# Second and third tile of each sequence: value product directly ahead of the next scores, output projection behind QKV, lower part of the output on GpSimd

## The chip, the core and the metric

The kernel runs on one core of one Trainium2 chip. The metric is the device time of one execution in microseconds (us), and several executions give a median. The engines are TensorE (PE in the rows; PEld are its weight loads), VectorE (DVE), ScalarE (ACT), GpSimd (POOL) and the DMA queues, of which SyncE (SP) issues nearly all.

## The reference

Eight sequences of 512 rows and 256 columns go through a two-layer transformer block, a linear recurrence (a fast-weight learner with a delta rule), and the same transformer block again. The change touches the transformer layers only, and there the attention half:

```python
def _layer(x, wqkv, qs, ksc, wo, lg, lb, w1, b1, w2, b2):
    h = shift_token(x)
    q, k, v = jnp.split(h @ wqkv, 3, axis=-1)        # 8 heads of 64
    q = l2norm(q) * qs
    k = l2norm(k) * ksc
    q, k = rotary_xpos(q, k)
    o = local_attention(q, k, v)                     # window 128, looks one window back
    x = x + o.transpose(0, 2, 1, 3).reshape(b, n, INNER) @ wo
    h = shift_token(x)
    h = layernorm(h) * lg + lb
    a, g = jnp.split(h @ w1 + b1, 2, axis=-1)
    x = x + (a * gelu(g)) @ w2 + b2
    return x
...
x = x + 0.5 * ffn(layernorm(x))
x = x + attn(layernorm(x))
x = x + 0.5 * ffn(layernorm(x))
```

## The kernel before

**Passes and tiles.** Four layer passes (two layers, run twice) go over eight sequences, so 32 sequence passes; between the second and the third layer stands the recurrence, which the change leaves alone. A sequence is four tiles of 128 rows, t = 0 to 3, called first to fourth tile here. Every large product is made with operands split into a high and a low part and three products (`split_product`, L1181): high by high, high by low, low by high.

**Order.** Nothing schedules the kernel: each engine has its own program, written out by hand in a function `sequence` (PE L1445, ACT L962, DVE L2073, POOL L686), and semaphores tie them. An engine does its steps strictly in that order, so an instruction that waits holds up all that stands behind it on its engine. While TensorE works on tile t of a sequence, it also prepares tile t+1 ("ahead") and the input of tile t+2, and between these steps it fills in the second feed-forward product of the sequence before (`W2`, 17 units of one 128x256 product for each tile, cut into pieces by the table `cuts`).

**TensorE, second to fourth tile.** Scores `S` (L1255, 48 products of 64x64 quarters of the array); output projection `WO` of the tile before (L1183 to L1185 with `wo`, 12 products into bank 6); QKV of the tile ahead, `A1` (18 products into banks 0, 1 and 2); transposes of the probabilities `PT` and `PTE` (L1275, L1282); 7 units of `W2` (L1441); transposes of the input, `A0` (L1195); the value product `PV` (L1306, 64 products on quarters of the array, into banks 6 and 4); transposes of q and k of the tile ahead, `A2` (L1228; q first, which waits for `qrot`, then k, which waits for `krot`); 10 units of `W2`. In the fourth tile `H2T` (L1345, L1351: transposes of the normalized rows) and the fourth `WO` follow, and then the first feed-forward product `W1`, 132 products.

**VectorE, second to fourth tile.** `W2` (L1999, the residual of the sequence before); `O` (L1907, the low part of the output of the tile before); `S` (L1879, the scores with mask, scale and row minimum), with the reciprocals `R`; for the tile ahead rotary and its sum for k (L1841, L1845, L1852) and the sum of squares of k (L1866); `WO` (L1914: adds the projection in bank 6 to the residual and releases `xa_done`, for which `PV` waits, since it writes bank 6 again); the sum of squares of q, rotary for q and its sum (L1852 again, which releases `qrot`); `halves` (L1933, L1934: statistics of the tile before); `A0` (L1817); `O_add` (L1901: adds the two halves of the value product). In the fourth tile `LN_moments` (L1949, L1947, L1953) and `halves` stand behind `WO`, ahead of the squares of q, and `LN_apply` (L1961, L1965), `O`, `W2`, `H2T` and `WO` of the fourth tile behind `O_add`.

**ScalarE** copies the transposed probabilities (L866, L875), the halves of the output (`O_first` L885) and its high part (`O` L899), q and k (L847, L835), and makes the exponentials (L856). **GpSimd** multiplies the probabilities with the reciprocals (`NP` L642) and k with its norm (`A1_k` L629, which releases `krot`), makes powers (L626, L637, L674), and adds the bias (`XB` L659).

## Time and profile before

| | us |
|---|---|
| median of 3 runs | 2507.77 (2507.73 to 2510.44) |
| the profiled execution | 2504.67 |
| its span, first to last instruction | 2502.8 |
| PE busy in it | 2460.8 (98%) |
| DVE busy | 1972.0 (79%) |
| ACT busy | 1813.8 (72%) |
| POOL busy | 1561.5 (62%) |

The granted clock of TensorE is 0.999 of its full 2.4 GHz over the span. A matmul's record is longer than the time it takes of the engine, since the products are pipelined: what counts is from one start to the next. A timeline row gives the start of a group of like instructions, its length, the number in it, and, in brackets, how long the engine had stood idle before it and what ended that.

### The profile page before, as it was taken

Reading aid. Unit: us, or ns where it says so; the run is one execution under the profiler, and the core shown is the slowest. Engines: PE = TensorE matmul, PEld = TensorE weight load, DVE = VectorE, ACT = ScalarE, POOL = GpSimd, SP = SyncE. Lnnn points to the kernel's source line nnn. Section 1 sums busy time; section 2 is a strip of 40 time slices with the busy share of each in tenths; the row PEclk is TensorE's granted clock in tenths of the full one; section 3 lists DMA queues with packets and bytes.
Section 4 is the critical chain, followed back from the end, with each engine's and each line's share of the span. In section 5 each row is a group of like instructions: output and inputs, shape, how many; then the busy total and the mean of one; then the engine's idle time right before and its main releaser. Section 6 shows DMA issues by size and latency. Waiting matters only on the chain. (4 is left out here: it accounts for less than half of the span.)

```text
span 2502.8 us, 80310 instructions
## 1 busy us (share of the span) xinstructions
PE 2460.8 (98%) x29664; PEld 2208.2 (88%) x29664; DVE 1972.0 (79%) x6501; ACT 1813.8 (72%) x5232; POOL 1561.5 (62%) x1799
## 2 busy tenths in 40 slices
PE   8999999999999999999999999999999999999999
PEld 7899989999999999998766899999999989999998
DVE  7788888877878887777656888777777788888886
ACT  6777777777777777776554777777777777777776
POOL 6566667666666676665212666666666667666665
PEclk9999999999999999999999999999999999999999
DMA  3121111003000000005101000000003100000000
GB/s 128 36 86 56 37 58 56 27 24 121 15 3 2 3 2 28 2 4 211 36 19 35 2 3 2 3 2 2 2 2 124 36 2 19 19 19 19 19 19 27
DMA packets 75957, 82.21 MB, mean 33 GB/s; under 512 B 37552, under 2 KB 61872, under 8 KB 74416
## 3 DMA queue, kind: packets, MB, share of 16 engines
q1 hardware_dynamic: 74272, 75.61, 9.3%
q8 instruction: 238, 3.90, 0.6%
q10 hardware_dynamic: 1296, 1.46, 0.2%
q14 instruction: 151, 1.24, 0.2%
HBM read 49.53 MB, written 26.74 MB: 30 GB/s over the span
## 5 line engine op out<-in xcount | busy, mean ns | idle before, releaser
L642 POOL TENSOR_TENSOR pr<-pr,rden 128x384 f32<-128x384 f32 (+1 forms) x480 | 409.4, 870 | 275.7 <-DVE rden L1888 270.4
L856 ACT ACTIVATE pr<-pr,nb 128x192 f32<-128x192 f32 (+1 forms) x1024 | 438.0, 430 | 169.7 <-DVE nb L1879 169.7
L1183 PE MATMUL bank<-h2T,w 128*128 128x256 f32 x1344 | 386.1, 287 | 2.7
L1184 PE MATMUL bank<-h2T,w 128*128 128x256 f32 x1344 | 376.8, 280 | 0.0
L1185 PE MATMUL bank<-h2T,w 128*128 128x256 f32 x1344 | 376.8, 280 | 0.0
L1879 DVE CUSTOM_DVE_ANT_0 pr<-bank,maskb,r 128x192 f32<-128x192 f32 (+1 forms) x1024 | 347.0, 393 | 25.9 <-POOL r L637 11.8
L684 POOL TENSOR_TENSOR uTl<-t,uTh 128x256 fp32r<-128x256 f32 x288 | 217.8, 760 | 182.3 <-ACT uTh L956 149.1
L1183 PE MATMUL bank<-wqkv,hT 128*128 128x512 f32 x768 | 304.5, 397 | 1.8 <-DVE nb L1879 1.8
L1184 PE MATMUL bank<-wqkv,hT 128*128 128x512 f32 x768 | 302.7, 394 | 0.0
L1185 PE MATMUL bank<-wqkv,hT 128*128 128x512 f32 x768 | 299.8, 390 | 0.0
L1983 DVE SCALAR_TENSOR_TENSOR t<-bank,b,t 128x256 f32<-128x256 f32 (+1 forms) x384 | 184.4, 480 | 108.5 <-POOL uTl L684 46.2
L1183 PEld LDWEIGHTS bank<-h2T,w 128*128 128x128 f32 x1344 | 253.9, 189 | 8.1 <-issue 5.8
L1184 PEld LDWEIGHTS bank<-h2T,w 128*128 128x128 f32 x1344 | 257.1, 191 | 0.0
L1185 PEld LDWEIGHTS bank<-h2T,w 128*128 128x128 f32 x1344 | 252.6, 188 | 0.0
L1441 PE MATMUL bank<-w2h,uTh 128*128 128x256 f32 (+1 forms) x768 | 225.6, 294 | 2.3 <-issue 2.3
L1441 PE MATMUL bank<-w2l,uTh 128*128 128x256 f32 (+1 forms) x768 | 224.9, 293 | 0.0
L674 POOL TENSOR_TENSOR rs<-vare,small 128x4 f32<-128x4 f32 (+2 forms) x96 | 95.1, 991 | 204.4 <-DVE vare L1953 204.2
L637 POOL TENSOR_TENSOR r<-ssg,small 128x8 f32<-128x8 f32 x128 | 213.1, 1665 | 10.7
L626 POOL TENSOR_TENSOR r<-ssg,small 128x8 f32<-128x8 f32 x128 | 213.2, 1665 | 8.0
L1255 PE MATMUL bank<-kT,qT 64*64 64x64 f32 (+2 forms) x6656 | 207.9, 264 | 6.4 <-ACT kT L835 3.1
L941 ACT ACTIVATE t<-bank,b 128x256 f32<-128x256 f32 x320 | 150.6, 471 | 81.2 <-PE bank L1185 77.8
L1255 PEld LDWEIGHTS bank<-kT,qT 64*64 64x64 f32 x6656 | 184.5, 133 | 25.6 <-ACT kT L835 5.4
(256 smaller groups left out, 7122.4 us busy)
## 6 DMA issues: line engine op xcount, KB each, us to landing
wqkv<-wqkv_split SPq DMA_DIRECT2D x18, 512.0 KB, 6.3
w<-w_split SPq DMA_DIRECT2D x3, 2816.0 KB, 9.8
Y<-in_x SPq DMA_DIRECT2D x8, 512.0 KB, 8.2
stt<-stt SPq DMA_DIRECT2D x256, 3.0 KB
out<-Y SPq DMA_DIRECT2D x8, 512.0 KB, 3.8
h<-out SPq DMA_DIRECT2D x7, 512.0 KB, 3.9
out<-h SPq DMA_DIRECT2D x7, 512.0 KB, 3.0
stt<-stt SPq DMA_DIRECT2D x192, 0.0 KB
```

The costliest lines, as they stand in the source:

```text
L626: e.tensor_tensor(r[:, t, 0, :], ssg[:, 0, :], minus_half, ALU.pow).then_inc(rk_done, 1)
L637: e.tensor_tensor(r[:, t, 1, :], ssg[:, 1, :], minus_half, ALU.pow).then_inc(rq_done, 1)
L642: e.tensor_tensor(probs(j, t), probs(j, t), rden[:, 2 * j:2 * j + 2].unsqueeze(2).to_broadcast([P, 2, w]), ALU.mult).then_inc(pn_done, 1 i ...
L684: e.tensor_tensor(uTl[:, half, JOBS[i], :], ut[:, job % 2, :], uTh[:, half, JOBS[i], :], ALU.subtract).then_inc(u_lo, 1)
L856: last = e.activation(probs(j, t)[:, g, :], probs(j, t)[:, g, :], ACT.Exp, bias=nb[:, hd:hd + 1], scale=-1.0, accum_out=den[:, hd:hd + 1])
L1183: e.matmul(out, left[0], right[0], start=first, stop=False)
L1184: e.matmul(out, left[0], right[1], start=False, stop=False)
L1185: return e.matmul(out, left[1], right[0], start=False, stop=last)
L1255: m = e.matmul(out[:, to:to + w, :], qT[rows, 0, p, HB * a:HB * a + HB], kT[rows, p, block:block + w, :], start=True, stop=True, skip_grou ...
L1441: mm = e.matmul(bank[bk][:, 0:D], left, right, start=(unit == 0), stop=(unit == UNITS - 1))
L1879: m = e.tensor_tensor_reduce(probs(j, t)[:, g, :], bank[j][:, g * 256:g * 256 + w], far, r[:, t, 1, place(hd):place(hd) + 1], FAR, ALU.add ...
L1983: e.scalar_tensor_tensor(ut[0:rows, job % 2, :], bank[job % 4][0:rows, 0:256], b1[0:rows, L % 2, 0, mt:mt + 1], gg[0:rows, job % 2, :], AL ...
```

## The change

It is made in the second and third tile (t = 1, 2) and, in part, in the fourth (t = 3).

- TensorE: `PV` of the second and third tile goes from ahead of `A2` to behind it, so that the next tile's scores follow it. The fourth stays where it is. `WO` of the second and third tile goes from ahead of QKV to behind it, ahead of `PT` (the first tile's stays ahead). The 17 units of `W2` are cut anew: second tile 17 between `PTE` and `A0` (before 7, and 10 behind `A2`); third tile 6 between scores and QKV and 11 behind `PTE`; fourth tile 6 between scores and QKV, 2 behind `PTE` and 9 behind `A2`.
- ScalarE: `O_first` of the second and third tile behind the copies of q and k.
- VectorE: `O_add` of the second and third tile from the end of its tile to the start of the next, where the low part `O` stood. `WO` of the second and third tile from ahead of the squares of q to behind the sum of rotary for q; `halves` of the third tile with it.
- GpSimd: new function `O_lower` makes the low part of the output of the second and third tile, ahead of `NP`.

```diff
@@ -673,6 +673,13 @@
                 e.wait_ge(s_pln, at(s_pln, 3 * b + (24 * L + part + 1)))
                 e.tensor_tensor(rs[:, half, lo:hi], vare[:, half, lo:hi], small[:, 0:1].to_broadcast([P, hi - lo]), ALU.pow).then_inc(rs_done, 1)
 
+            def O_lower(L, b, t):
+                n = idx(L, b, t)
+                for i in pair:
+                    e.wait_ge(o_hi, at(o_hi, 2 * n + i + 1))
+                    e.tensor_tensor(oT[:, 1, 2 * i:2 * i + 2, :].rearrange("p a c -> p (a c)"), o_sum[:, 2 * P * i:2 * P * i + 2 * P],
+                                    oT[:, 0, 2 * i:2 * i + 2, :].rearrange("p a c -> p (a c)"), ALU.subtract).then_inc(o_lo, 1)
+
             def zero_rest():
 
                 e.memset(uTh[:, :, MT - 1, :].bitcast(F32), 0.0).then_inc(s_zero, 1)
@@ -690,6 +697,8 @@
                         XB(*prev, t)
                     if prev and t == 0:
                         U_last(*prev)
+                    if t > 1:
+                        O_lower(L, b, t - 1)
                     for j in range(4 if t else 3):
                         if t == 0 and j == 2:
                             guard_k(*ahead)
@@ -979,13 +988,14 @@
                         PTE(L, b, t)
                     if ahead2:
                         A0(*ahead2)
-                    if t:
+                    if t == 3:
                         O_first(L, b, t)
-                    if t == 3:
                         O(L, b, t)
                     if ahead and t:
                         A2_q(*ahead)
                         A2_k(*ahead)
+                        if t < 3:
+                            O_first(L, b, t)
                     elif ahead:
                         A2_k(*ahead)
                         A2_q(*ahead)
@@ -1446,7 +1456,7 @@
                 for t in range(NT):
                     ahead = (L, b, t + 1) if t < NT - 1 else nxt and (*nxt, 0)
                     ahead2 = (L, b, t + 2) if t < NT - 2 else nxt and (*nxt, t - 2)
-                    cuts = ((5, 6, 11, 13, UNITS), (0, 0, 7, UNITS), (0, 0, 7, UNITS), (0, 0, 7, UNITS))[t]
+                    cuts = ((5, 6, 11, 13, UNITS), (0, 0, UNITS, UNITS), (0, 6, UNITS, UNITS), (0, 6, 8, UNITS))[t]
 
                     def fill(k):
                         if prev and cuts[k] < cuts[k + 1]:
@@ -1456,8 +1466,8 @@
                         W2(*prev, t, 0, cuts[0])
                     S(L, b, t, 0, bool(nxt))
                     S(L, b, t, 1, bool(nxt))
-                    if t:
-                        WO(L, b, t - 1)
+                    if t == 1:
+                        WO(L, b, 0)
                     fill(0)
                     if L == 0 and b == 0 and t:
                         beta((5, 4, 6)[t - 1])
@@ -1466,6 +1476,8 @@
                     else:
                         e.wait_ge(nb_done, at(nb_done, 4 * idx(L, b, t) + 1))
                         busy(14, 0)
+                    if t > 1:
+                        WO(L, b, t - 1)
                     for j in range(4):
                         if not ahead and j > 1:
                             busy(4, 0)
@@ -1475,13 +1487,15 @@
                     fill(1)
                     if ahead2:
                         A0(*ahead2)
-                    if t:
+                    if t == 0:
+                        PV_first(L, b, t)
+                    if t == 3:
                         PV(L, b, t)
-                    else:
-                        PV_first(L, b, t)
                     if ahead and t:
                         A2(*ahead, 1)
                         A2(*ahead, 0)
+                        if t < 3:
+                            PV(L, b, t)
                     elif ahead:
                         A2(*ahead, 0)
                         fill(2)
@@ -2076,8 +2090,11 @@
                     ahead2 = (L, b, t + 2) if t < NT - 2 else nxt and (*nxt, t - 2)
                     if prev and t:
                         W2(*prev, t - 1)
-                    if t:
-                        O(L, b, t - 1)
+                    if t == 1:
+                        O(L, b, 0)
+                    elif t:
+                        for i in pair:
+                            O_add(L, b, t - 1, i)
                     S(L, b, t, 0)
                     S(L, b, t, 1)
                     S(L, b, t, 2)
@@ -2110,22 +2127,24 @@
                         if ahead:
                             rotated(*ahead, 0)
                             squares(idx(*ahead), 0)
-                        WO(L, b, t - 1)
+                        if t == 1:
+                            WO(L, b, 0)
                         if t == 3:
                             LN_moments(L, b, 0)
-                            halves(L, b, t - 1)
                         if ahead:
                             squares(idx(*ahead), 1)
                             rotary(*ahead, 1)
                             rotated(*ahead, 1)
                         if L == 0 and b == 0 and t == 3:
                             beta()
-                        if t < 3:
-                            halves(L, b, t - 1)
+                        if t > 1:
+                            WO(L, b, t - 1)
+                        halves(L, b, t - 1)
                         if ahead2:
                             A0(*ahead2)
-                        for i in pair:
-                            O_add(L, b, t, i)
+                        if t == 3:
+                            for i in pair:
+                                O_add(L, b, t, i)
                     if L == 0 and b < 2 and t == 1:
                         entry_stats(b + 1, 2)
                         entry_stats(b + 1, 3)
```

The names in the order rows are the program's: bank is PSUM, `ident,t` the transposes of q (waits `qrot`) and k (waits `krot`), `pT,v` the value product, `kT,qT` the scores, w2h, w2l, uTh, uTl the units of `W2`.

TensorE in the second tile of a sequence of the first layer, behind the transposes of the input, before:

```order
L1306 MATMUL bank<-pT,v 64x128 [waits pt_sb,xa_done]
L1306 MATMUL bank<-pT,v 64x128 x7
L1306 MATMUL bank<-pT,v 64x128 [waits pt_sb]
L1306 MATMUL bank<-pT,v 64x128 x7
L1306 MATMUL bank<-pT,v 64x64 [waits pt_sb]
L1306 MATMUL bank<-pT,v 64x64 x15
L1228 MATMUL bank<-ident,t 128x128 [waits qrot]
L1228 MATMUL bank<-ident,t 128x128 x3
L1228 MATMUL bank<-ident,t 128x128 [waits krot]
L1228 MATMUL bank<-ident,t 128x128 x3
L1441 MATMUL bank<-w2l,uTh 128x256
L1441 MATMUL bank<-w2h,uTl 128x256
```

And in the changed kernel, at the same place:

```order
L1238 MATMUL bank<-ident,t 128x128 [waits qrot]
L1238 MATMUL bank<-ident,t 128x128 x3
L1238 MATMUL bank<-ident,t 128x128 [waits krot]
L1238 MATMUL bank<-ident,t 128x128 x3
L1316 MATMUL bank<-pT,v 64x128 [waits pt_sb,xa_done]
L1316 MATMUL bank<-pT,v 64x128 x7
L1316 MATMUL bank<-pT,v 64x128 [waits pt_sb]
L1316 MATMUL bank<-pT,v 64x128 x7
L1316 MATMUL bank<-pT,v 64x64 [waits pt_sb]
L1316 MATMUL bank<-pT,v 64x64 x15
L1265 MATMUL bank<-kT,qT 64x192 [waits qt_sb,kt_sb]
L1265 MATMUL bank<-kT,qT 64x128
```

The value product has changed places with the transposes, no unit of `W2` is left behind them, and the scores of the third tile follow the value product.

VectorE in the fourth tile, from the squares of k to the sum of rotary for q (Y is the residual, stt the statistics, mv the moments), before:

```order
L1866 TENSOR_REDUCE ssk<-sq 128x8 [waits k_and_q_guarded,sqk]
L1914 TENSOR_TENSOR Y<-bank,Y 128x256 [waits wo_ps]
L1949 BN_AGGR mv<-stt 128x2 [waits st_moved0]
L1949 BN_AGGR mv<-stt 128x2
L1947 BN_AGGR mv<-stt 128x2 x2
L1953 TENSOR_SCALAR vare<-mv 128x4 [waits rs_done,mv_done]
L1933 BN_STATS stt<-Y 128x6 [waits xa_done]
L1934 BN_STATS stt<-Y 128x6
L1866 TENSOR_REDUCE ssq<-sq 128x8 [waits k_and_q_guarded,sqq]
L1841 TENSOR_TENSOR t<-bank,rot 128x512 [waits qt_ps,q_ps]
L1845 TENSOR_TENSOR t<-bank,rot 128x512
L1852 TENSOR_TENSOR t<-t 128x512 [waits rotq]
```

And in the changed kernel:

```order
L1880 TENSOR_REDUCE ssk<-sq 128x8 [waits k_and_q_guarded,sqk]
L1963 BN_AGGR mv<-stt 128x2 [waits st_moved0]
L1963 BN_AGGR mv<-stt 128x2
L1961 BN_AGGR mv<-stt 128x2 x2
L1967 TENSOR_SCALAR vare<-mv 128x4 [waits rs_done,mv_done]
L1880 TENSOR_REDUCE ssq<-sq 128x8 [waits k_and_q_guarded,sqq]
L1855 TENSOR_TENSOR t<-bank,rot 128x512 [waits qt_ps,q_ps]
L1859 TENSOR_TENSOR t<-bank,rot 128x512
L1866 TENSOR_TENSOR t<-t 128x512 [waits rotq]
L1928 TENSOR_TENSOR Y<-bank,Y 128x256 [waits wo_ps]
L1947 BN_STATS stt<-Y 128x6 [waits xa_done]
L1948 BN_STATS stt<-Y 128x6
```

The addition to Y (which waits `wo_ps`) and the two statistics behind it now stand behind the last row of q instead of ahead of its first.

GpSimd from the power for q to the power for k, in the third tile, before:

```order
L637 TENSOR_TENSOR r<-ssg,small 128x8 [waits nb_done,k_and_q_guarded]
L659 TENSOR_TENSOR xb<-Y,b 128x256 [waits xf_done,xa_done]
L642 TENSOR_TENSOR pr<-pr,rden 128x384 [waits rden_done] x4
L616 TENSOR_SCALAR ssg<-ssk 128x8 [waits ssk_done]
L626 TENSOR_TENSOR r<-ssg,small 128x8 [waits k_and_q_guarded]
```

And in the changed kernel:

```order
L637 TENSOR_TENSOR r<-ssg,small 128x8 [waits nb_done,k_and_q_guarded]
L659 TENSOR_TENSOR xb<-Y,b 128x256 [waits xf_done,xa_done]
L680 TENSOR_TENSOR oT<-qT,oT 128x256 [waits o_hi] x2
L642 TENSOR_TENSOR pr<-pr,rden 128x384 [waits rden_done] x4
L616 TENSOR_SCALAR ssg<-ssk 128x8 [waits ssk_done]
L626 TENSOR_TENSOR r<-ssg,small 128x8 [waits k_and_q_guarded]
```

Two subtractions of 128x256 stand between the bias and the probabilities, and wait for the high part (`o_hi`).

## Rows read from the trace of the kernel before

**Rows 1.** The page's first part: busy us, share of the span, instructions.

```profile
PE 2460.8 (98%) x29664; PEld 2208.2 (88%) x29664; DVE 1972.0 (79%) x6501; ACT 1813.8 (72%) x5232; POOL 1561.5 (62%) x1799
```

**Rows 2.** Timeline of PE, one fourth tile: start, length in us, instruction, number.

```profile
851.85 1.68 PE L1255 MATMUL bank<-kT,qT 64*64 64x192 f32 x48
...
861.24 0.38 PE L1195 MATMUL bank<-ident,Y 128*128 128x128 f32 x2
861.55 1.57 PE L1306 MATMUL bank<-pT,v 64*64 64x128 f32 x64
863.25 1.09 PE L1228 MATMUL bank<-ident,t 128*128 128x128 f32 x8
...
865.51 0.63 PE L1351 MATMUL bank<-ident,h 128*128 128x128 f32 x4
866.00 0.35 PE L1183 MATMUL bank<-wo,oT 128*128 128x256 f32 x1
```

**Rows 3.** Timeline of DVE, the same fourth tile.

```profile
853.06 0.40 DVE L1879 CUSTOM_DVE_ANT_0 pr<-bank,maskb,r 128x192 f32<-128x192 f32 x1
...
858.70 0.69 DVE L1866 TENSOR_REDUCE ssk<-sq 128x8 f32<-128x512 f32 x1
859.31 0.42 DVE L1914 TENSOR_TENSOR Y<-bank,Y 128x256 f32<-128x256 f32 x1
859.64 0.27 DVE L1949 BATCH_NORM_AGGREGATE mv<-stt 128x2 f32<-128x12 f32 x2
...
860.16 0.28 DVE L1933 BATCH_NORM_STATS2 stt<-Y 128x6 f32<-128x128 f32 x1
...
860.56 0.67 DVE L1866 TENSOR_REDUCE ssq<-sq 128x8 f32<-128x512 f32 x1
...
862.46 0.74 DVE L1852 TENSOR_TENSOR t<-t 128x512 f32<-128x512 f32 x1
863.12 0.41 DVE L1817 TENSOR_TENSOR hT<-bank,hT 128x256 fp32r<-128x256 f32 x1
...
864.40 1.11 DVE L1965 TENSOR_SCALAR h<-Y,mv,rs 128x128 f32<-128x128 f32 x4
```

**Rows 4.** Timeline of POOL, the same fourth tile.

```profile
861.61 1.04 POOL L629 TENSOR_TENSOR t<-t,r 128x512 f32<-128x512 f32 x1
```

**Rows 5.** Timeline of DVE, the end of the third tile.

```profile
850.26 0.76 DVE L1901 TENSOR_TENSOR qT<-bank,qT 128x256 f32<-128x256 f32 x2 [0.50 <-ACT qT L885]
```

**Rows 6.** Timeline of PE, second tile from 834, last value products of the third.

```profile
834.44 0.38 PE L1195 MATMUL bank<-ident,Y 128*128 128x128 f32 x2
...
838.12 0.28 PE L1441 MATMUL bank<-w2h,uTh 106*128 106x256 f32 x1
838.24 0.28 PE L1441 MATMUL bank<-w2l,uTh 106*128 106x256 f32 x1
...
838.45 1.68 PE L1255 MATMUL bank<-kT,qT 64*64 64x192 f32 x48
...
849.48 0.24 PE L1306 MATMUL bank<-pT,v 64*64 64x64 f32 x4
849.65 0.33 PE L1228 MATMUL bank<-ident,t 128*128 128x128 f32 x1
```

**Rows 7.** Timelines of DVE and POOL, second tile (834, 835) and third.

```profile
834.99 0.69 DVE L1852 TENSOR_TENSOR t<-t 128x512 f32<-128x512 f32 x1
...
835.06 1.53 POOL L629 TENSOR_TENSOR t<-t,r 128x512 f32<-128x512 f32 x1
...
848.27 0.69 DVE L1852 TENSOR_TENSOR t<-t 128x512 f32<-128x512 f32 x1
...
848.33 1.53 POOL L629 TENSOR_TENSOR t<-t,r 128x512 f32<-128x512 f32 x1
```

**Rows 8.** Timelines of POOL and DVE where POOL starts first, an earlier sequence.

```profile
171.49 0.73 POOL L684 TENSOR_TENSOR uTl<-t,uTh 128x256 fp32r<-128x256 f32 x1 [1.25 <-ACT uTh L956]
...
171.59 0.91 DVE L1988 TENSOR_TENSOR uTh<-t,uTh 42x256 fp32r<-42x256 f32 x1
```

## Prediction

> **What bounds the kernel now.** I read the page's busy shares first: TensorE is busy for 98% of the span [rows 1], so a change pays only if it shortens the row of TensorE's starts, or closes one of its few gaps. Then I read TensorE's timeline, start to start, in one pass over a sequence, and beside it VectorE and GpSimd for the semaphores that its next step needs. The 32 passes are near copies of each other, so one stands for all. All times of the fourth tile are given as +x us from its first score product (851.85).
>
> Two things are to be seen. First, changes of product shape cost TensorE a little. A unit of the second feed-forward product takes 0.12 (838.12 to 838.24), but the last one is followed by the scores only after 0.21; the last four value products are followed by the transposes after 0.17 [rows 6], where such groups elsewhere in the 1.50 us of 64 products come at under 0.1. Each such border costs about 0.1. Second, in the fourth tile VectorE is as late as TensorE: the value product runs from +9.70 to +11.20 (64 products in 1.50), and the transposes of q start only at +11.40 [rows 2], when the sum of rotary for q, started at +10.61, is done [rows 3]. That chain has no slack.
>
> **What the change gives.** In the second and third tile the borders from `W2` to the scores and from the value product to the transposes go, and one from the value product to the scores comes. Both of these use 64x64 quarters of the array. If that border is free, the last value product is followed by the scores after 0.06 instead of 0.17.
>
> The Trainium skill, page "TensorEngine Tiling (Array Packing)", section "Key Properties", says that a change of tiling mode, not of tile, drains TensorE. By it this border is free, and by the other end it costs another 0.11. No row has a value product ahead of scores.
>
> *Second tile.* Ten units of `W2` (0.117 each) now stand ahead of the input's transposes, so these start at 834.44 + 1.17 = 835.61, those of q at 835.83, and those of k could start at 836.32 (four transposes in 0.49, as in the 865.51 row [rows 2]). But k is released by GpSimd's product, which ends at 835.06 + 1.53 = 836.59 [rows 7]; nothing ahead of it on VectorE or GpSimd changes in this tile. So k starts at 836.65, a wait of 0.33 that the value product used to cover. Three more transposes (0.33), the border (0.20, as from 861.24 to 861.55 less one transpose [rows 2]), and 1.33 of value products bring us to 838.51; the scores start 0.06 to 0.17 later, 838.57 to 838.68, against 838.45 [rows 6]: **+0.12 to +0.23**.
>
> *Third tile.* The same sum without the wait. The addition of the projection (0.33) leaves VectorE's chain ahead of q, so its two-input sum starts at 848.27 - 0.33 + 0.10 = 848.04 (0.10 is the later start of the scores' work, below) and GpSimd's product, which stood behind it from 848.33 [rows 7], ends about 0.23 earlier, at 849.63. The transposes of q start at 849.23, of k at 849.72, the value product at 850.25, and the scores at 851.64 to 851.75, against 851.85: **-0.21 to -0.10**. The 6 units between scores and QKV and the 12 projection products behind QKV are only moved. Together the two tiles make -0.09 to +0.13 a pass, -3 to +4 us in 32. I take -3, the free border.
>
> *The start of VectorE's work on the scores.* It now waits for `O_add`, which waits for ScalarE's `O_first`, which waits for the value product. From the end of that to the addition it took 0.61 (849.65 to 850.26 [rows 5, 6]); two additions are 0.70, and the scores start 0.10 sooner behind the last product. So VectorE starts on them at +1.41 instead of +1.21 [rows 3]. TensorE's QKV needs the first bank at about +2.4, by when its two heads (0.68) are read: hidden by the scores and 6 units. The high part on ScalarE ends before the first exponential, and the subtractions on GpSimd (two of 0.73, the length of such an op [rows 8]) lie in the time in which GpSimd waits for the first reciprocal. The projection that needs them is behind QKV. I cost them at nothing; if a subtraction held up the probabilities by 0.5, the later `PT` (0.7 behind its old place) would still cover it.
>
> **What the change costs: the fourth tile.** TensorE gets to the value product at +9.70 + 0.12 = +9.82 (8 units stand ahead of it instead of 7). But the value product writes bank 6, and waits until VectorE has added the third tile's projection. Before, that addition ran at +7.46 [rows 3], two microseconds early. Now it stands behind the sum for q. The chain, with durations of [rows 3]: squares of k at +6.85 + 0.20 = +7.05; 0.61 later the moments, at +7.66; these take 0.52 (859.64 to 860.16), +8.18; from the squares of q to the sum is 1.90 (860.56 to 862.46), so the sum starts at **+10.08**, though addition and statistics (0.33 + 0.40) are out of its way.
>
> At that moment GpSimd reads the same port or not: its product for k started at +9.76 [rows 4], now +9.96, and ends at +11.00. Two-input operations of VectorE and GpSimd exclude each other in this trace. Where VectorE started 0.06 to 0.07 ahead, GpSimd's took 1.53 [rows 7] instead of 1.04 [rows 4]. Where GpSimd started 0.10 ahead, a VectorE operation 256 wide took 0.91 [rows 8], against 0.42 for an addition of the same width [rows 3], and went on 0.14 before GpSimd's row ended. Here GpSimd is 0.12 ahead, so I take the second: VectorE goes on at +10.86, the sum takes 0.60 and the addition 0.42 (+11.88), and the value product starts at **+11.93**, a wait of 2.1 us.
>
> The Trainium skill, page "SBUF — State Buffer", section "Who interferes with whom", has the same: the pair of ports is an exclusive lock, issue order decides who blocks, and a VectorE instruction with two SBUF inputs contends with a GpSimd one that reads SBUF. The trace agrees (1.53 against 1.04).
>
> What follows the value product follows VectorE: the additions, then the normalization, whose last piece ended 3.96 behind the start of the value product (865.51 against 861.55 [rows 2, 3]). So now +15.89; the last transpose of the normalized rows comes 0.05 later, and the fourth projection 0.16 after it, at +16.10, against +14.15 (866.00 [rows 2]). TensorE's 9 units of `W2` are done by then. Fourth tile: **+1.95**. The feed-forward part behind it starts later by as much, and holds no slack that gives it back, since TensorE was the bound there. Two of the 32 passes prepare no tile ahead and have no such chain: 30 x 1.95 = 58.5.
>
> **Sum.** 58.5 - 3 = +55.5; 2504.67 + 55.5 = 2560.2. The median of the runs is 3.1 above the profiled execution: **2563**.
>
> **Rivals.**
> 1. *VectorE is first at the port.* GpSimd's lead of 0.12 rests on five steps of 0.02 accuracy each, and where the line lies between 0.10 ahead and 0.06 behind is not shown. Then the sum runs from +10.08, the addition ends at +11.10, the value product starts at +11.15, the fourth projection at +15.32: +1.17, 35 us in 30 passes, less 3: 2540. For it: the closeness. Against it: the case of [rows 8].
> 2. *Some passes go one way, some the other*: 2545 to 2558.
> 3. *The chain is not late (the other side).* If the addition is done by +9.76, the fourth tile costs one unit (0.12), and if GpSimd's k is early in the second tile too, both give 0.21: -0.30 a pass, 2498. It needs VectorE's chain to come 1.3 us sooner than its rows add up to; the only thing that pulls it is QKV, which is done 0.7 earlier, and that alone doesn't do, since the chain starts with reciprocals that wait for ScalarE's exponentials.
> 4. *More comes behind it.* The statistics of the third tile go to their neighbours by DMA 3.6 us later, while the instruction of VectorE that needs them moves by 1.95; if they were only just in time, up to 1.6 is lost, and half of it, 0.8 in 30 passes, gives 2580 or more. The trace shows no wait of this kind in the fourth tile.
>
> **How the numbers follow.** Forecast 0.55 (2554 to 2572 with the border and 0.2 a pass on the chain); rival 1 0.20 (2533 to 2547); rival 2 0.08; rival 3 0.07; rival 4 0.07; a smaller loss or none 0.03. From 2534 to 2578 holds about 0.83. Faster by over 0.2% (about what a measurement of this kernel tells from no change) is rival 3, 0.07; within 0.2% 0.02; slower 0.91.
>
> **What the profile after would show.** The value product of the fourth tile with an idle time of 2.1 us (1.3 for rival 1) ahead of it, put down to VectorE's addition to Y; the sum for q in the fourth tile with a row of about 1.4 us instead of 0.74; second tile 0.1 to 0.2 longer with a wait for GpSimd ahead of k; third tile shorter by 0.1 to 0.2; the scores 0.06 or 0.17 behind the last value product. I am wrong if the addition ends before +9.8, or if the fourth tile's loss comes back in the feed-forward part.

## The result and the profile after

The changed kernel takes **2599.26 us** (median of 4 runs, 2592.62 to 2600.38), beside 2508.68 (2507.73 to 2510.44) for the kernel before in the same series: ratio 1.035, 95% interval 1.034 to 1.037. It is slower, by 91 us, where 55 were forecast; 2599 lies above the range's 2578. The profiled execution took 2599.59, span 2597.8, against 2504.67 and 2502.8.

The page's busy shares of the changed kernel, answering [rows 1]:

```profile
PE 2483.7 (96%) x29664; PEld 2230.4 (86%) x29664; DVE 1948.4 (75%) x6373; ACT 1829.0 (70%) x5232; POOL 1642.2 (63%) x1927
```

The same 29664 products, TensorE busy for 23 us more and idle for 72 us more. VectorE is busy for 24 us less, GpSimd for 81 more.

The fourth tile of an undisturbed pass of the changed kernel, timelines of PE, DVE and POOL, answering [rows 2 to 4] (start, length in us; the tile's scores start at 2408.92):

```profile
2408.92 1.63 PE L1265 MATMUL bank<-kT,qT 64*64 64x192 f32 x48
...
2418.39 0.38 PE L1205 MATMUL bank<-ident,Y 128*128 128x128 f32 x2
2420.85 1.57 PE L1316 MATMUL bank<-pT,v 64*64 64x128 f32 x64 [2.08 <-DVE Y L1928]
2422.35 1.09 PE L1238 MATMUL bank<-ident,t 128*128 128x128 f32 x8
...
2425.29 0.36 PE L1193 MATMUL bank<-wo,oT 128*128 128x256 f32 x1
```

```profile
2419.02 1.45 DVE L1866 TENSOR_TENSOR t<-t 128x512 f32<-128x512 f32 x1
2420.39 0.41 DVE L1928 TENSOR_TENSOR Y<-bank,Y 128x256 f32<-128x256 f32 x1
...
2424.73 0.76 DVE L1921 TENSOR_TENSOR oT<-qT,oT 128x256 fp32r<-128x256 f32 x2
```

```profile
2418.87 1.04 POOL L629 TENSOR_TENSOR t<-t,r 128x512 f32<-128x512 f32 x1
```

GpSimd's product starts at +9.95, VectorE's sum for q 0.15 behind it, at +10.10; its row is 1.45 instead of 0.74 (the distance is 0.14 to 0.15 and the row 1.44 or 1.45 in all 30 passes); the addition starts at +11.47 and the value product at **+11.93**, 2.08 late. Forecast were +9.96, +10.08, +11.46 and +11.93. The fourth projection starts at +16.37, not at +16.10: it waits for VectorE's low part of the fourth output (L1921), whose first half ends at 2425.15. The list of waits (us in total, times, longest) shows that this is the same in every pass that has the chain:

```profile
PEld bank L1316 <- DVE Y L1928: 72.7, 30, 3.1
...
PE bank L1316 <- DVE Y L1928: 65.6, 30, 2.9
```

30 waits give 65.6 us, and the longest is 2.9: some are longer than 2.08. Two things stand in the trace that the forecast did not have. The first is TensorE's clock. The windows of the changed kernel around the value product of another fourth tile (start:end, busy us and count of PE, PEld, DVE, ACT, POOL, then the granted clock), and its PE rows:

```profile
302.00:306.00 4.00, 1.42 (x13) 1.18 (x11) 3.93 (x10) 2.98 (x8) 3.75 (x4) 1.00 0.02 6
306.10:309.50 3.40, 3.37 (x67) 3.25 (x68) 0.81 (x3) 0.40 (x2) 2.40 (x3) 0.50 0.04 2
309.60:313.00 3.40, 3.40 (x31) 3.29 (x30) 3.09 (x12) 2.52 (x7) 0.00 (x0) 1.00 0.26 77
...
306.13 2.84 PE L1316 MATMUL bank<-pT,v 64*64 64x128 f32 x64 [2.72 <-DVE Y L1928]
308.90 1.36 PE L1238 MATMUL bank<-ident,t 128*128 128x128 f32 x8
```

TensorE was busy for 1.42 of the 4 us ahead. Then, in the stretch in which it works again, its clock is granted at 0.50 (1.2 GHz), and behind that at 1.00 (2.4 GHz). The 64 value products take 2.77 from start to start instead of 1.50. The trace before has one such stretch between its start and its end, and none in a fourth tile; the one of after has 17, and 14 of them fall on the value product of a fourth tile or the transposes behind it, each in another of the 32 passes. Of the other three, one stands at the border of the first two passes as in the trace before, one in the second tile of the seventeenth pass, and one in the recurrence. An undisturbed pass takes 72.5 (before 70.3), one with such a stretch 73.7.

The second is ScalarE. Timeline of ACT in the changed kernel, from the third to the fourth tile of the third sequence in the first layer:

```profile
218.49 0.66 ACT L894 ACTIVATE qT<-bank 128x256 f32<-128x256 f32 x2 [0.99 <-PE bank L1316]
219.43 0.72 ACT L908 ACTIVATE oT<-qT 128x256 fp32r<-128x256 f32 x2 [0.28 <-DVE qT L1915]
220.06 1.08 ACT L1038 ACTIVATE Y<-Y,off,rs 128x256 f32<-128x256 f32 x2
221.04 0.44 ACT L865 ACTIVATE pr<-pr,nb 128x192 f32<-128x192 f32 x1
```

L1038 is `entry_apply`, the normalization of the next sequence's input, in the first layer alone. It stands behind `O` of the second and third tile. With the value product, `O` has moved to directly ahead of the exponentials (L865), so 1.08 us of other work now delays them. In the five passes that have it (the third to seventh), the fourth tile's value product starts at +12.58 or +12.59 instead of +11.93, and four of the five show waits of 2.72 to 2.75 there.

The second tile, timelines of PE and POOL:

```profile
1734.90 0.38 PE L1205 MATMUL bank<-ident,Y 128*128 128x128 f32 x2
1735.12 0.60 PE L1238 MATMUL bank<-ident,t 128*128 128x128 f32 x4
1735.91 0.66 PE L1238 MATMUL bank<-ident,t 128*128 128x128 f32 x4 [0.19 <-POOL t L629]
1736.50 1.57 PE L1316 MATMUL bank<-pT,v 64*64 64x128 f32 x64
1737.89 0.39 PE L1265 MATMUL bank<-kT,qT 64*64 64x192 f32 x4
```

```profile
1734.33 1.53 POOL L629 TENSOR_TENSOR t<-t,r 128x512 f32<-128x512 f32 x1
```

The transposes of k start 0.79 behind those of q instead of 0.41 to 0.44, when GpSimd's product ends. The scores come 1.39 behind the start of the value product and 0.04 behind its last one; before, the transposes came 1.50 behind its start. That border is free.

### The profile page after: what moved, and what is told of

It reads as the page before. It is cut to its first block and busy times, and to the rows that moved or that the text cites. A ratio compares the mean times of both kernels' runs of the same rounds, so it can differ in the third digit from the quotient of the medians.

```text
span 2597.8 us, 80310 instructions
## 1 busy us (share of the span) xinstructions
PE 2483.7 (96%) x29664; PEld 2230.4 (86%) x29664; DVE 1948.4 (75%) x6373; ACT 1829.0 (70%) x5232; POOL 1642.2 (63%) x1927
## 5 line engine op out<-in xcount | busy, mean ns | idle before, releaser
L865 ACT ACTIVATE pr<-pr,nb 128x192 f32<-128x192 f32 (+1 forms) x1024 | 437.8, 430 | 75.1 <-DVE nb L1893 75.1
L674 POOL TENSOR_TENSOR rs<-vare,small 128x4 f32<-128x4 f32 (+2 forms) x96 | 95.3, 993 | 285.2 <-DVE vare L1967 285.0
L1451 PE MATMUL bank<-w2h,uTh 128*128 128x256 f32 (+1 forms) x768 | 233.2, 304 | 2.8 <-issue 2.8
L1316 PE MATMUL bank<-pT,v 64*64 64x128 f32 (+1 forms) x6144 | 163.1, 259 | 66.4 <-DVE Y L1928 65.6
L1316 PEld LDWEIGHTS bank<-pT,v 64*64 64x64 f32 x6144 | 148.7, 143 | 85.2 <-DVE Y L1928 72.7
L1451 PE MATMUL bank<-w2l,uTh 128*128 128x256 f32 (+1 forms) x768 | 218.3, 284 | 0.0
```

Source lines behind the costliest of these rows:

```text
L865: last = e.activation(probs(j, t)[:, g, :], probs(j, t)[:, g, :], ACT.Exp, bias=nb[:, hd:hd + 1], scale=-1.0, accum_out=den[:, hd:hd + 1])
L1316: return e.matmul(bank[O_BANK[a]][64 * g:64 * g + 64, j * P + lo:j * P + lo + right.shape[-1]], v[64 * a:64 * a + 64, tile, hd * DH:(hd + ...
L1451: mm = e.matmul(bank[bk][:, 0:D], left, right, start=(unit == 0), stop=(unit == UNITS - 1))
```

## Experiments

Line numbers of the kernels differ by a few. Times are medians; each series had its own runs of the kernel before (2507.3 to 2508.3).

### The wait undone, and the wait alone

The first puts VectorE's addition back in the changed kernel; the second makes only that addition late in the kernel before.

```diff
@@ the changed kernel, VectorE @@
-                        if t == 1:
-                            WO(L, b, 0)
+                        if t != 2:
+                            WO(L, b, t - 1)
                         if t == 3:
                             LN_moments(L, b, 0)
+                            halves(L, b, t - 1)
...
@@ the kernel before, VectorE @@
-                        WO(L, b, t - 1)
+                        if t < 3:
+                            WO(L, b, t - 1)
                         if t == 3:
                             LN_moments(L, b, 0)
-                            halves(L, b, t - 1)
...
+                        if t == 3:
+                            WO(L, b, t - 1)
+                        halves(L, b, t - 1)
```

> The changed kernel, with VectorE's addition of the third tile's projection and its statistics (in the fourth tile alone) put back where they stood, ahead of the squares of q. If the late addition is what holds the value product, the 2.1 us of idle time ahead of it go: TensorE starts it about 0.2 behind the transposes of the input, waits for up to 0.5 inside it for ScalarE's last probability copies, and q's transposes start about 1.6 us sooner than in the changed kernel. 30 x 1.6 = 48 us, and the stretches at a granted clock of 0.5, which all begin at this idle time, go too (another 15 to 20 us). That gives 2525 to 2540. Rival, that the loss comes from the work that GpSimd now does for the projection: it is still there, so the time stays over 2580.

Measured: **2526.13** (2524.03 to 2531.30), ratio 1.008, interval 1.006 to 1.009. 73 of the 91 us are gone, and no low stretch falls in a fourth tile.

> The kernel before, with one edit: in the fourth tile VectorE adds the third tile's projection and takes its statistics behind the sum for q, not ahead of the squares of q. No part of the change's order of products, and nothing of its work on GpSimd. By the theory this alone makes most of the loss: the sum for q starts at +9.88, 0.12 behind GpSimd's product for k (+9.76), is held until +10.66 and shows a row of about 1.4 us; the value product starts at +11.7 instead of +9.70, the fourth tile gets 2.0 longer in 30 passes (60 us), and the idle time of about 2.0 us brings stretches at a granted clock of 0.5 (15 us): 2583 (2576 to 2590). If the loss needs the change's other parts, the time stays under 2550. If only the low clock stays away, 2568.

Measured: **2583.16** (2582.50 to 2587.45), ratio 1.031, interval 1.029 to 1.032. DVE and POOL of this kernel, fourth tile (scores at 1810.31):

```profile
1820.22 1.45 DVE L1852 TENSOR_TENSOR t<-t 128x512 f32<-128x512 f32 x1
1821.59 0.41 DVE L1914 TENSOR_TENSOR Y<-bank,Y 128x256 f32<-128x256 f32 x1
```

```profile
1820.08 1.04 POOL L629 TENSOR_TENSOR t<-t,r 128x512 f32<-128x512 f32 x1
```

A row of 1.45 again, and low stretches in 11 fourth tiles. The place of one addition of 0.41 us, and of the statistics that go with it, costs the kernel before 76 us. Neither the order of products nor GpSimd's new work is needed for it.

### What holds VectorE: the port

```diff
@@ the changed kernel, VectorE @@
-                        if t == 3:
-                            LN_moments(L, b, 0)
...
                         if t > 1:
                             WO(L, b, t - 1)
+                        if t == 3:
+                            LN_moments(L, b, 0)
```

GpSimd's power for the moments (L674) goes behind its power for q.

> The changed kernel, with VectorE's moments of the first half (0.52 us, fourth tile) moved from ahead of the squares of q to behind the addition of the projection, and GpSimd's power for them behind its power for q. The sum for q then starts at about +9.56 of the tile instead of +10.12, 0.4 ahead of GpSimd's product for k. If the row of 1.45 us of that sum is a wait for the port that GpSimd holds, it falls to 0.6 to 0.75, the addition ends at about +10.6 to +10.7, and the idle time ahead of the value product falls from 2.1 to about 0.9: 1.2 x 30 = 36 us, and some or all of the 15 to 20 us of the low clock: about 2548 (2540 to 2565). If the long row has another cause, it stays at 1.45 and only the 0.55 of the earlier start is won: 2583. If GpSimd's product gets in between the sum and the addition, the addition's row becomes the long one (1.2 instead of 0.41), and the time is 2575 to 2585.

Measured: **2564.35** (2561.29 to 2566.42), ratio 1.023, interval 1.021 to 1.024. DVE, POOL and PE of its fourth tile (scores at 2372.80):

```profile
2382.38 0.69 DVE L1866 TENSOR_TENSOR t<-t 128x512 f32<-128x512 f32 x1
2382.99 0.42 DVE L1928 TENSOR_TENSOR Y<-bank,Y 128x256 f32<-128x256 f32 x1
```

```profile
2382.78 1.20 POOL L629 TENSOR_TENSOR t<-t,r 128x512 f32<-128x512 f32 x1
```

```profile
2383.46 1.57 PE L1316 MATMUL bank<-pT,v 64*64 64x128 f32 x64 [0.77 <-DVE Y L1928]
...
2387.56 0.35 PE L1355 MATMUL bank<-lead,pick 128*128 128x2 f32 x2 [0.45 <-DVE h L1979]
```

With VectorE 0.40 ahead, its row is 0.69 in this fourth tile, as in the 30 of the run that have the chain, and GpSimd's is the longer one (1.20). So the 1.45 was the port, and who is first decides. The value product starts at +10.66, as expected, 1.27 sooner. But an undisturbed pass is only 0.5 shorter (72.0): the moments now come late, and TensorE waits for the normalization instead (0.45 at L1355). That makes 15 of the 35 us; most of the rest is the clock, which is at full speed up to the last 2 us of the span.

The Trainium skill, page "SBUF — State Buffer", section "Who interferes with whom", calls this port pair an exclusive lock in which issue order decides; the two traces agree, 1.45 against 1.04 one way and 0.69 against 1.20 the other.

### The clock by itself

The first fills the wait with 16 more products of one unit, so its output is another one; the second moves nine real units into it.

```diff
@@ TensorE, t == 3 @@
+                        if ahead and prev:
+                            repeated(16, *prev, t)
                         PV(L, b, t)
...
@@ the other kernel @@
-... (0, 6, 8, UNITS))[t]
+... (0, 6, UNITS, UNITS))[t]
```

> The changed kernel, with 16 more products of 128x256 (the term of one unit of the second feed-forward product, again and again, so the output is another one) ahead of the fourth tile's value product: TensorE works for 1.9 of the 2.1 us in which it waited for VectorE. Nothing else is changed, and the value product still starts when VectorE's addition is done. If the stretches at a granted clock of 0.5 follow from this idle time, they go, the value product takes 1.50 in every pass, and the kernel is 15 to 20 us faster than the changed kernel: 2580 to 2585. If they have another cause, or cost nothing, the time stays at 2599.

Measured: **2583.10** (2579.40 to 2587.40), 16 us below the changed kernel.

> The changed kernel, with the nine units of the second feed-forward product that stand behind q's and k's transposes in the fourth tile moved ahead of the transposes of the input. They fill 1.05 of the 2.1 us of idle time ahead of the value product; the value product starts as before, and behind k's transposes TensorE waits for VectorE's normalization instead. If half the idle time still brings the stretches at 0.5, the time stays at 2599; if they need the long idle time, 2580 to 2585, but the new idle time behind k's transposes (about 1.1) can bring them back at another place. That the fourth tile gets shorter by itself is not expected: the chain on VectorE is the same.

Measured: **2585.19** (2583.88 to 2585.63), 14 below. Rows of the kernel with 16 more products, around the same place as above; windows and PE:

```profile
302.00:305.10 3.10, 2.27 (x20) 2.06 (x18) 3.03 (x6) 1.96 (x6) 2.96 (x3) 1.00 0.01 3
305.10:308.50 3.40, 3.39 (x81) 3.32 (x82) 2.08 (x9) 1.42 (x5) 2.38 (x3) 1.00 0.04 2
...
305.11 1.57 PE L1316 MATMUL bank<-pT,v 64*64 64x128 f32 x64 [0.84 <-DVE Y L1935]
306.61 1.09 PE L1238 MATMUL bank<-ident,t 128*128 128x128 f32 x8
```

The clock is 1.00 behind the wait and the value product takes 1.50. In both kernels it still waits for the same addition, and an undisturbed pass is 72.4 to 72.5 as in the changed kernel: nothing else got shorter. So the low clock costs about **15 us** of the 91. In the second kernel an idle time of about 1.03 is left ahead of the value product (1.64 to 1.67 where ScalarE's normalizations stand in the way), and the clock holds there in every pass but the first. In the first pass, which has no units to fill with, the wait is 2.86 in both kernels, and the low stretch comes in both.

### ScalarE's two normalizations

```diff
@@ ScalarE @@
                         A2_k(*ahead)
+                        if L == 0 and 1 < b < B - 1 and t < 3:
+                            for k in (2 * t - 2, 2 * t - 1):
+                                entry_apply(b + 1, k)
                         if t < 3:
                             O_first(L, b, t)
```

> The changed kernel, with ScalarE's two normalizations of the next sequence's rows (1.08 us together; first layer, third to seventh sequence, second and third tile) put ahead of the copies of the value product instead of between them and the exponentials. ScalarE is idle for about 1.0 there. If they are what makes the third and fourth tile of those passes about 0.66 longer each, 5 passes get 1.3 us shorter: 6 us less than the changed kernel, 2593, and the segments of these passes read as those of the later layers. If they only follow another delay, nothing changes in those passes.

Measured: **2593.86** (2590.20 to 2596.59), 5.4 below the changed kernel. The third tile's transposes of q and k take 1.02 in these passes again instead of 1.49, and the value product of the fourth is reached 0.66 sooner (2.44 behind the input's transposes instead of 3.10), as in the other layers. The runs of the two kernels overlap; these segments don't.

### The wait for k in the second tile: two misses

First three units between the transposes of q and k, then half the value product.

```diff
@@ TensorE, t == 1 @@
                         A2(*ahead, 1)
+                        if t == 1:
+                            fill(2)
                         A2(*ahead, 0)
...
@@ the other kernel @@
                         A2(*ahead, 1)
+                        if t == 1:
+                            PV(L, b, t, 0)
                         A2(*ahead, 0)
```

> The changed kernel, with three of the seventeen units of the second feed-forward product, in the second tile, moved from ahead of the transposes of the input to between those of q and those of k: they fill the 0.33 us in which TensorE waits there for GpSimd's product. The second tile gets 0.33 shorter in each of 32 passes: 10 us less than the changed kernel, 2589. If something else is as late as GpSimd's product (VectorE's addition, the value product's probabilities), the wait only moves behind k and the time stays at 2599.

Measured: **2599.51** (2595.99 to 2602.76), no change. PE and POOL of its second tile:

```profile
1732.59 0.66 PE L1238 MATMUL bank<-ident,t 128*128 128x128 f32 x4
...
1733.49 0.65 PE L1238 MATMUL bank<-ident,t 128*128 128x128 f32 x4
```

```profile
1731.91 1.53 POOL L629 TENSOR_TENSOR t<-t,r 128x512 f32<-128x512 f32 x1
```

k starts at 1733.49, 0.05 behind the end of GpSimd's product, and 3.10 behind the first unit as in the changed kernel. The end of the wait is fixed by GpSimd; units taken from ahead of it only open the same gap elsewhere (q is reached sooner, and waits for VectorE). My expectation was wrong in its logic: only work from behind the wait can fill it. So I tried that, on top of the addition back and the early normalizations:

> The changed kernel with VectorE's addition back and ScalarE's normalizations early (as in the one with three edits, without its split of the units, which gave nothing), and in the second tile the first 32 products of the value product, which stood behind k, put between the transposes of q and those of k. They are work from behind k and not from ahead of it, so they fill the 0.33 us in which TensorE waits for GpSimd, less two borders of 0.05 to 0.1: 0.15 to 0.25 a pass, 5 to 8 us: 2515 to 2518. If the wait for k were not what sets the end of the second tile, the time stays at 2523 or rises by the borders.

Measured: **2529.66** (2529.46 to 2531.08), 7 slower than the kernel with three edits (2523.08, below), not 5 to 8 faster. PE of its second tile:

```profile
1758.43 0.60 PE L1241 MATMUL bank<-ident,t 128*128 128x128 f32 x4
1758.96 1.10 PE L1319 MATMUL bank<-pT,v 64*64 64x128 f32 x32
1760.00 0.66 PE L1241 MATMUL bank<-ident,t 128*128 128x128 f32 x4
1760.58 0.69 PE L1319 MATMUL bank<-pT,v 64*64 64x64 f32 x32
1761.34 0.56 PE L1268 MATMUL bank<-kT,qT 64*64 64x192 f32 x8
```

```profile
1760.69 0.60 ACT L844 ACTIVATE kT<-bank 128x512 f32<-128x512 f32 x1 [1.02 <-PE bank L1241]
```

GpSimd was done at 1759.17, so k waited for nothing. The two borders cost about 0.1 each, near what I had put them at: the first half takes 1.04 up to k, where it takes 0.92 up to the second half in the changed kernel, and the border behind q costs 0.09. What I had left out is ScalarE. It copies k only when k's transposes are done, and now only half of the value product covers that copy: it ends at 1761.29, and the scores, which need it, come 0.76 behind the second half instead of 0.46. The sum is 2.91 from q to the scores, against 2.77 in the changed kernel (1735.12 to 1737.89). That is 4 us in 32 passes. Another 2.5 lie in the third tile of the five passes with ScalarE's normalizations (0.5 each); no run here takes that part by itself.

### What is left with the addition back

All three edits at once, then the projection of the fourth tile ahead of QKV, fewer units ahead of QKV, and the addition at yet another place.

> The changed kernel with three edits at once: VectorE's addition of the third tile's projection back ahead of the squares of q, three units between q's and k's transposes in the second tile, and ScalarE's two normalizations ahead of the copies. The first alone gave 2526; the second takes 10 off and the third 4 to 6: about 2511 (2507 to 2515). What is then left against the kernel before is the wait inside the fourth tile's value product for ScalarE's last probability copies (2.25 instead of 1.62), which come 0.7 later because the projection stands behind QKV. If the pieces were not independent, the sum fails by more than 4.

Measured: **2523.08** (2521.75 to 2525.86), ratio 1.006, interval 1.005 to 1.008: 3 below the addition back alone, with overlapping runs. The split units gave nothing again (second tile 0.01 to 0.02 shorter). The normalizations shorten the third tile of the five passes by 0.67 each, as in the changed kernel, and give less in the fourth.

```diff
@@ TensorE, on top of the three edits @@
+                    if t == 3:
+                        WO(L, b, 2)
                     if ahead:
                         A1(*ahead)
```

> As the one with three edits, and in the fourth tile TensorE's projection of the third tile's output stands between the six units and QKV instead of behind QKV (GpSimd's subtractions are to be done at about +3.2 of the tile, when its second half needs them). The probabilities are transposed at the same time, but the projection is no longer between QKV and them. If that is what makes ScalarE's copies late, the value product takes 1.6 again instead of 2.25: 30 x 0.6 = 18 us less, about 2493 (2488 to 2500), and below the kernel before. If GpSimd's subtractions are late, or QKV's later start (0.8) makes k and q late on VectorE, the loss moves there and the time is 2505 or more.

Measured: **2536.20** (2532.98 to 2540.22), ratio 1.011. The value product falls only to 2.13, and QKV comes later. A row of DVE in its fourth tile (scores at 1712.15):

```profile
1717.78 0.69 DVE L1862 TENSOR_TENSOR t<-bank,rot 128x512 f32<-128x512 f32 x1 [0.51 <-PE bank L1198]
```

Rotary for k waits 0.51 for QKV; the rival of the expectation holds.

> The changed kernel with VectorE's addition back and ScalarE's normalizations early, and in the fourth tile four units instead of six between the scores and QKV (two more behind k's transposes). With the addition back, VectorE waited 0.40 at it for the projection, which TensorE ends at about +8.0 behind QKV, and everything behind it came 0.40 later: q's transposes at +12.05 against +11.40 before. Two units less bring QKV and the projection 0.24 sooner, and ScalarE's copies too; VectorE's two first heads are read by +2.1, when QKV now starts. q's transposes come at about +11.7, 0.35 sooner: 30 x 0.35 = 10 us below the 2523 of the one with three edits, 2511 to 2516. If GpSimd's probabilities are not ready at +7.7, nothing is won: 2523.

Measured: **2522.88** (2522.21 to 2525.49), no gain. PE of its fourth tile (scores at 1770.91), the start of QKV:

```profile
1773.21 0.47 PE L1196 MATMUL bank<-wqkv,hT 128*128 128x512 f32 x1
```

QKV starts 0.07 sooner than it did, not 0.24, and its 18 products take 4.22 instead of 4.16: it waits for VectorE to read the banks of the scores, which starts 0.2 later than before the change. It ends when it did.

```diff
@@ VectorE, t == 3, on top of the four units @@
                             squares(idx(*ahead), 1)
+                        if t == 3:
+                            WO(L, b, t - 1)
```

> As the one with four units, but VectorE's addition of the projection stands behind the squares of q (and its statistics behind the sum for q), so that it waits for nothing. The sum for q is then ready at about +10.4, while GpSimd reads the port from +9.96 to +11.0: by the rule of the long row (1.45) it is held until +10.9 and ends at +11.5, so q's transposes come at +11.6, as in the one with four units: the same time within 4 us, 2510 to 2516, with a row of about 1.1 to 1.2 for the sum. If the port did not hold it, it would be 0.5 sooner on VectorE, and TensorE would only wait for ScalarE's copies. A time under 2507 would beat the kernel before.

Measured: **2538.79** (2536.70 to 2543.10), 16 slower than the one with four units. DVE and the DMA queue of SyncE from its fourth tile into the feed-forward part:

```profile
1792.39 1.12 DVE L1869 TENSOR_TENSOR t<-t 128x512 f32<-128x512 f32 x1
...
1798.71 0.42 DVE L1931 TENSOR_TENSOR Y<-bank,Y 128x256 f32<-128x256 f32 x1 [0.65 <-DMA stt<-stt]
```

```profile
1793.93 0.64 SPq L409 DMA_DIRECT2D stt<-stt  x1
...
1797.05 0.64 SPq L416 DMA_DIRECT2D stt<-stt  x1
```

The sum's row is 1.12 with GpSimd 0.47 ahead, as the port demands, and q's transposes come 0.28 sooner, though the fourth projection doesn't (+14.71 in both). And the third tile's statistics are 2.5 later than with four units, their five DMAs are issued one after the other until 1797.7, and VectorE's last addition of the sequence waits for them (0.65 here, 0.45 to 0.92 in the 30 passes), and with it the second half of the normalization. This is the mechanism of the prediction's fourth rival. In the changed kernel that addition (L1928 at 2427.05) waits for TensorE instead: the last of the five DMAs is issued by 2424.93, and with the 1.02 that pass here between the end of its issue and the addition, an estimate, it would be done 1.1 ahead. From the fourth tile's scores to the next sequence it is 0.3 longer than with four units in most passes, and 0.5 to 2.2 in eight of the first nine, for which no cause is shown.

No kernel here beats the one before.

## Why the prediction was too small

**Right.** What bounds the kernel, the direction, and the mechanism: the fourth tile's value product waits 2.08 for an addition that stands behind the sum for q, and that sum is held by GpSimd's product, 0.15 ahead. Every step up to the value product is within 0.02. In all 30 passes GpSimd was first at the port, so rivals 1 and 2 fall, and the kernel with the moments behind shows the other order. The lead of 0.12 rested on five steps of 0.02 each, so hitting its side was in part luck, as the chance of 0.20 for rival 1 says. The wait for k (k 0.36 later behind q than its transposes take, 0.33 forecast), the free border, and the second and third tile (+0.17 and -0.22 a pass from scores to scores, forecast +0.12 to +0.23 and -0.21 to -0.10) are right too or within 0.01, and GpSimd's subtractions, costed at nothing, show no wait behind them.

**Wrong, three terms, all of one sign.**

| term | forecast | measured |
|---|---|---|
| fourth tile, 30 passes | 58.5 | 67 (2.23 each) |
| second and third tile | -3 | -2 |
| TensorE's clock | 0 | 15 |
| ScalarE's normalizations | 0 | 5 |
| sum | 55.5 | 85 |
| the medians | | 91 |

1. *The step from the value product to the fourth projection.* I rebuilt it from VectorE's end of the normalization, plus 0.05 and 0.16: 4.17. The end (+15.89) and the last transpose behind it (+15.95) came as forecast. But the projection waits for neither. It waits for VectorE's low part of the fourth output, which stands behind the normalization and which I left out. Its first half takes 0.42 and ends at 2425.15, and the projection follows 0.15 later. In the kernel before the same row stood there:

```profile
865.43 0.75 DVE L1907 TENSOR_TENSOR oT<-qT,oT 128x256 fp32r<-128x256 f32 x2
```

Its first half ended at 865.85, and the projection started at 866.00, again 0.15 later. So in both kernels this row sets the start of the projection, and the length of the way from the value product to it stood in the rows: 4.45 from start to start (861.55 to 866.00 [rows 2]), and 4.44 after the change. Carrying it over would have given +16.38, against +16.37 measured: 0.28 in 30 passes, 8 us.
2. *The clock.* I priced the wait as idle time alone. The products behind it are slower too, in 14 passes. Nothing in the trace before shows such a wait in the middle of a pass, so its price was unknown, and it should have been bounded all the same: at worst the 64 products take twice their 1.50 and k's and q's transposes twice their 0.85, 2.3 in 30 passes, 70 us on top. The range had no room for it at all.
3. *`entry_apply`.* It stands behind `O` in ScalarE's program. I moved `O` past everything that the diff shows, and not the step that follows it, which the diff doesn't show: it stood in idle time of ScalarE, and now stands ahead of the exponentials. The prediction costed the start of the work on the scores at nothing; in these five passes the third tile gets 0.65 longer by it and the fourth 0.4, 5 us in all.

With these the sum is 2508.68 + 85 = 2594, inside the spread of the four runs (2592.6 to 2600.4). About 3 of the other 6 us are the clock again, outside the fourth tiles. The second tile of the seventeenth pass takes 15.13 with its low stretch and 13.79 in the kernel with the moments behind, which has none there. The stretch from the last scores ahead of the recurrence to the first behind it takes 235.49 against 233.95. The rest was not pursued.

**What stays with the addition back** (19 us over the kernel before) is told by the trace of that kernel: the projection stands behind QKV, so VectorE waits for it at the addition, and ScalarE's probability copies are 0.6 later. PE and DVE, fourth tile (scores at 1777.86):

```profile
1787.66 1.10 PE L1316 MATMUL bank<-pT,v 64*64 64x128 f32 x32
1789.00 0.69 PE L1316 MATMUL bank<-pT,v 64*64 64x64 f32 x32 [0.24 <-ACT pT L884]
1789.91 1.09 PE L1238 MATMUL bank<-ident,t 128*128 128x128 f32 x8 [0.21 <-DVE t L1866]
```

```profile
1786.00 0.42 DVE L1928 TENSOR_TENSOR Y<-bank,Y 128x256 f32<-128x256 f32 x1 [0.40 <-PE bank L1195]
```

The transposes of q start at +12.05 instead of +11.40. A pass is 0.55 longer, 16 us in 30. That the late projection is the cause is read from these rows; the two kernels meant to shorten it failed at other waits, so it isn't shown by an experiment.

## What to carry to other kernels

Where a chain on a helper engine ends exactly when the main engine needs it, a short operation moved from its front to its end costs the whole chain, and a port that two engines share can double a step of it (0.74 to 1.45 here); work out who starts first, and look at the steps that the diff doesn't show but that stand behind a moved one. Price a wait of TensorE with what comes behind it, the clock included. For each later step ask what it waits for, and check the sum against the distance from start to start that the rows have. A wait is filled only by work from behind it, and that gains only if nothing else leaned on the work that was moved: here half of a value product left ScalarE's copy of k uncovered.

## What the runs showed of the hardware

- Behind a wait of 1.9 to 2.9 us ahead of the fourth tile's value product, the granted clock of the stretch behind it was 0.50 in 14 of the changed kernel's 30 passes with that wait, and behind one of 1.9 to 3.1 us in 11 of the 30 of the kernel before with the late addition; in the other passes it stayed at 1.00 behind waits of the same length. With 0.5 to 1.7 us of idle time in the same place it stayed at 1.00 in all 58 such passes of the kernel with the moments behind and the kernel with nine units moved; the one fourth tile of these two that was hit had a wait of 2.86. It cost about 15 us here, some 1.2 for each pass that it hit (73.7 against 72.5).
- A two-input operation of VectorE that starts 0.14 to 0.15 behind one of GpSimd takes 1.45 instead of 0.69, the same in two kernels; 0.47 behind it takes 1.12; 0.40 ahead of it 0.69, with GpSimd at 1.20 instead of 1.04. Each of these is the same, within 0.01, in all 30 passes of its kernel.
- Between products on quarters of the array and full ones, TensorE's next start came 0.15 to 0.20 behind the last one (0.20 from the value product to k in the kernel that splits it), against 0.11 between products of one kind; from the value product to the scores, both on quarters, it came after 0.04. The Trainium skill, page "TensorEngine Tiling (Array Packing)", section "Key Properties", says that a change of mode drains the engine and a change of tile doesn't; by that rule the border between value product and scores was to be free, and the trace agrees.
